# Adding a group's shared column back one group later, and running a graph network's three stages without barriers or queued weights between them

## The reference

```python
h = jnp.maximum(_layernorm(x), 0.0)
e_h = rel_embed[rel_id]
for W_r, W_sl, W_el in [(W_r1, W_sl1, W_el1), (W_r2, W_sl2, W_el2)]:
    self_msg = jnp.where(iso_mask[:, None], h @ W_el, h @ W_sl)
    agg = jax.ops.segment_sum((e_h + h[src]) @ W_r, dst, num_segments=3125)
    h = rrelu(agg * norm + self_msg)
x = x + h
h = jnp.maximum(_layernorm(x), 0.0)
qk, v = h @ Wqk + bqk, h @ Wv + bv
scores = jnp.clip(jnp.sum(qk[dst] * qk[src], axis=-1) / sqrt(128), -5.0, 5.0)
attn = segment_softmax(scores, dst)
out = jax.ops.segment_sum(attn[:, None] * v[src], dst, num_segments=3125) @ Wo + bo
x = x + gamma * layernorm(out + h) + beta
```

## Time and profile before

| | us |
|---|---|
| median of three runs | 870.51 (868.87 to 872.46) |
| the profiled execution | 870.01 |
| its span in the trace | 868.3 |
| TensorE busy | 732.6 |
| VectorE busy | 527.7 |
| ScalarE busy | 431.5 |
| GpSimd busy | 245.1 |

### The profile page before, as it was taken

The page is one execution under the profiler, slowest core; times in us unless marked ns, Lnnn a source line. Parts: engine busy times, 40 slices in busy tenths (PEclk is TensorE's granted clock), DMA queues, the critical chain, the costliest instruction groups (busy, mean ns, idle before and its releaser), DMA issues. The chain is left out here.

```text
span 868.3 us, 15380 instructions
## 1 busy us (share of the span) xinstructions
PE 732.6 (84%) x5767; PEld 545.2 (63%) x5767; DVE 527.7 (61%) x931; ACT 431.5 (50%) x1085; POOL 245.1 (28%) x273
## 2 busy tenths in 40 slices
PE   4266698898889898977399999859999999999993
PEld 3255587788778788866289999824444444444463
DVE  4987997786768677541033333414476767666676
ACT  0445765564555555551011111237767676767661
POOL 6130010000001111100000000026666666666662
PEclk9999799799989999987699999979999999999996
DMA  4100200033300000011311111130000000000000
GB/s 130 33 1 18 59 2 7 23 103 71 100 9 7 8 8 7 8 60 61 108 31 37 36 37 37 37 106 1 1 4 21 3 22 2 24 0 24 2 25 18
DMA packets 39763, 27.89 MB, mean 32 GB/s; under 512 B 5311, under 2 KB 38163, under 8 KB 39686
## 3 DMA queue, kind: packets, MB, share of 16 engines
q1 hardware_dynamic: 39206, 26.35, 10.5%
q10 hardware_dynamic: 480, 0.53, 0.2%
HBM read 13.28 MB, written 10.80 MB: 28 GB/s over the span
## 5 line engine op out<-in xcount | busy, mean ns | idle before, releaser
L1462 POOL TENSOR_TENSOR counts<-counts,work 125x500 f32<-125x500 f32 x150 | 162.3, 1082 | 97.5 <-DVE work L1526 84.1
L1016 PE MATMUL sums<-work 125*128 125x196 f16 (+15 forms) x1220 | 157.1, 256 | 24.7 <-DVE work L825 24.6
L1384 PE MATMUL a_ps_o<-work 125*128 125x500 f32 (+1 forms) x350 | 159.2, 545 | 7.1 <-DVE work L1530 6.7
L1526 DVE SCALAR_TENSOR_TENSOR work<-a_ps_s,counts 125x500 f32<-125x500 f32 x150 | 101.6, 677 | 93.5 <-ACT a_ps_s L1482 93.4
L1372 PE MATMUL a_ps_s<-work 128*125 128x500 f32 x300 | 152.0, 589 | 6.9 <-PEq L534 6.9
L819 DVE TENSOR_TENSOR work<-work,counts 125x3024 f16<-125x3024 f16 (+1 forms) x60 | 114.3, 1906 | 65.5 <-PE sums L1018 62.4
L1477 ACT ACTIVATE a_ps_s<-a_ps_s,work 125x500 f32<-125x500 f32 (+1 forms) x157 | 102.1, 650 | 86.5 <-PE a_ps_s L1372 83.4
L1018 PE MATMUL sums<-work 125*128 125x10 f16 (+15 forms) x800 | 133.7, 196 | 0.0
L1187 ACT CAST counts<-sums 128x364 f32 (+38 forms) x305 | 131.9, 472 | 2.1 <-issue 1.4
L977 PE MATMUL sums<-counts 125*128 125x250 f16 (+1 forms) x975 | 124.5, 275 | 10.0 <-ACT work L1129 10.0
L825 DVE TENSOR_TENSOR work<-work,counts 125x4200 f16<-125x4200 f16 (+15 forms) x120 | 125.5, 1086 | 0.0
(11 more groups left out here) (178 smaller groups left out, 703.3 us busy)
## 6 DMA issues: line engine op xcount, KB each, us to landing
first_columns<-counts SPq DMA_DIRECT2D x5, 610.4 KB
counts<-first_columns SPq DMA_DIRECT2D x5, 610.4 KB
counts<-counts SPq DMA_DIRECT2D x5, 468.8 KB
counts<-in_x SPq DMA_DIRECT2D x5, 312.5 KB
h_nodes<-counts SPq DMA_DIRECT2D x5, 312.5 KB
work<-in_x SPq DMA_DIRECT2D x12, 125.0 KB
x_after_messages<-work SPq DMA_DIRECT2D x12, 125.0 KB
h_attention<-work SPq DMA_DIRECT2D x12, 125.0 KB
```

The source lines that it names most:

```text
L1016: pe.matmul(win[:, 0:c, cols], lo[:, k * 2 * LO:k * 2 * LO + 128], m[:, k, h0 * w:(h0 + c) * w].rearrange("p (h d) -> p h d", d=w), start= ...
L1384: last = pe.matmul(ps_o[c % 2][:, 0:cols(u) // n], h3[:, j + i, :], pbuf[u % PB][:, i * NP:i * NP + cols(u) // n], start=j + i == 0, stop= ...
L1462: pool.tensor_tensor(a, a, p, ALU.add).then_inc(acc_done, 1)
L1526: dve.scalar_tensor_tensor(pbuf[u % PB], ps_s[u % 4][0:NP, 0:WIDE], float(np.exp(-CLIP)), counts[0:NP, j, c * WIDE:(c + 1) * WIDE], ALU.ma ...
```

## The change

There are two parts. **One:** on TensorE, `add_back(g - 1)` now stands behind the tiles of group g and ahead of that group's slots. ScalarE's loop, the slots and the waits for banks are as before. **Two:** the stages are joined. There is one program block and one PSUM tensor instead of two; attention's functions are called inside the first block. The last chunks of layer one are written in another order, chunk 11 has its own banks and `ht`, the two halves of each split are interleaved, and the rows from DRAM are asked for one batch earlier. The start of layer two's first chunk is done ahead of layer one's last `agg`. The weights of layer two are issued by ScalarE, and the five reloads of `counts` by SyncE behind each of layer two's first five chunks. Scores 0 to 3 and the first units start before the last chunk's rows are finished; `last_turn` and `last_qk` stand behind units 1 and 3.

```diff
@@ TensorE, groups
                     if q == n - 1:
                         last.then_inc(ring_free, 1)
+                    if g:
+                        add_back(g - 1)
                     for step in slots[g]:
                         layer1(*step)
-                    pe.wait_ge(carry_ready, g + 1)
-                    for win, h0, h1 in wins:
-                        last = pe.matmul(win[:, :, 0:1], ident_h[:, :], carry[:, g % 2, h0:h1, None], start=False, stop=True, skip_group_check=True)
-                    last.then_inc(summed, 1)
@@ TensorE, behind the groups
-            for step in slots[GROUPS]:
-                layer1(*step)
+            add_back(GROUPS - 1)
+            for kind, c in (("own", DIRECT + 1), ("agg", DIRECT), ("sum", DIRECT + 1), ("self", DIRECT + 1),
+                            ("rest", DIRECT + 1), ("own", LAST), ("agg", DIRECT + 1), ("sum", LAST), ("self", LAST), ("rest", LAST)):
+                for step in by_kind.pop((kind, c)):
+                    layer1(*step)
+            own(0, ORDER2[0])
+            sums(0, ORDER2[0], 0, EARLY).then_inc(early, 1)
+            layer1("agg", LAST, 0)
...
-            h3_turn(LAST, ORDER2[LAST])
-            qk(LAST, ORDER2[LAST])
+            pe.wait_ge(L["rows"], LAST)
+            A["tensor_first"](pe)
...
+            A["tensor"](pe, last_turn, last_qk)
@@ SyncE
-            sp.wait_ge(ring_free, len(BATCHES))
+            sp.wait_ge(ring_free, len(BATCHES) - 1)
...
-            sp.wait_ge(sums_done, CHUNKS)
-            for i in range(5):
-                v = slice(5 * i, 5 * i + 5)
-                sp.dma_start(counts[0:NP, v, 0:HEAD], heads.rearrange("p (j d) -> p j d", d=HEAD)[:, v, :]).then_inc(heads_in, 16)
...
-            for t, v in zip((wr, ws[:, 0:D], ws[:, D:]), weights2):
-                sp.dma_start(t, v).then_inc(L["wts"], 16)
...
                 sp.dma_start(h3[:, c * LB * D:(c + 1) * LB * D], xc.rearrange("p b f -> p (b f)")).then_inc(L["h3_out"], 16)
+                if i < 5:
+                    v = slice(5 * i, 5 * i + 5)
+                    sp.dma_start(counts[0:NP, v, 0:HEAD], heads.rearrange("p (j d) -> p j d", d=HEAD)[:, v, :]).then_inc(heads_in, 16)
@@ ScalarE, ahead of layer two
+            act.wait_ge(agg_done, CHUNKS)
+            for t, v in zip((wr, ws[:, 0:D], ws[:, D:]), weights2):
+                act.dma_start(t, v).then_inc(L["wts"], 16)
+            act.dma_start(wqk, wqk_d).then_inc(L["wts"], 16)
+            act.dma_start(bqk, bqk_d.rearrange("(p o) -> p o", o=1)).then_inc(L["wts"], 16)
@@ ScalarE, behind layer two
+            A["scalar_first"](act)
             act.wait_ge(L["x2_ready"], CHUNKS)
@@ attention, TensorE: unit u
+            if u == 1:
+                last_turn()
+            if u == 3:
+                last_qk()
```

More of the change, by code:

```diff
@@ L326, in messages @@
     hn_in = [sem(f"hn_in{i}") for i in range(4)]
[L327 removed]
+    rounded2, parts2_ready = ([sem(f"{n}{i}") for i in range(2)] for n in ("rounded2_", "parts2_ready"))
+    early = sem("early")
     slots, at_slot = plan()
@@ new lines, in score @@
+    def score(pe, u):
+        c, j, n = units[u]
+        if u == NB - 1:
+            pe.wait_ge(T["rows"], -(-NB // 2))
+        out = ps_s[u % 4]
+        if c < FULL:
+            last = pe.matmul(out[0:NP, :WIDE], qk_t[:, j * NP:(j + 1) * NP], qk_t[:, c * WIDE:(c + 1) * WIDE], start=True, stop=True)
+        else:
+            for i in range(n):
+                last = pe.matmul(out[0:NP, i * NP:(i + 1) * NP], qk_t[:, (j + i) * NP:(j + i + 1) * NP], qk_t[:, FULL * WIDE:], start=True, stop=True)
+        last.then_inc(scores, 1)
@@ new lines, in below, with exponent, scalar_first @@
+    def below(act, u):
+        act.wait_ge(scores, u + 1)
+        s = ps_s[u % 4][0:NP, 0:cols(u)]
+        act.activation(s, s, ACT.Relu, bias=five, scale=-float(D) ** -0.5).then_inc(limited, 1)
+    def exponent(act, u):
+        act.wait_ge(limited, u + 1)
+        s = ps_s[u % 4][0:NP, 0:cols(u)]
+        act.activation(s, s, ACT.Exp, bias=five, scale=-1.0).then_inc(exped, 1)
+    def scalar_first(act):
+        act.wait_ge(consts, 2)
+        below(act, 0)
+        below(act, 1)
+        exponent(act, 0)
@@ new lines, in run_scalar, with take @@
+    def run_scalar(act, last_turned, last_rows):
+        def take(c):
+            act.wait_ge(pv_done, end_unit(c))
+            if c:
+                act.wait_ge(f_done, c)
+            w = blocks(c) * NP
+            act.copy(hv[:, 0:w], ps_o[c % 2][:, 0:w]).then_inc(hv_out, 1)
+        for u, (c, j, n) in enumerate(units):
+            if 0 < u < len(units) - 1:
+                below(act, u + 1)
+            if u:
+                exponent(act, u)
+            if u == 1:
+                last_turned()
+            if u == 3:
+                last_rows()
+            if c == 0 and j == 14:
+                act.wait_ge(wv_turned, 1)
+                act.copy(wv_t, ps_f[:, 0:D]).then_inc(wv_t_out, 1)
+            if c == 0 and j == 17:
+                act.wait_ge(wvo_done, 1)
+                act.copy(wvo, ps_f[:, D:2 * D]).then_inc(wvo_out, 1)
+                act.copy(bvo, ps_f[0:NP, 2 * D:3 * D]).then_inc(wvo_out, 1)
+            if 0 < c < FULL and j == 1 or c == FULL and j == 0:
+                take(c - 1)
+        take(FULL)
```

639 lines of the change are left out of this document (325 added, 314 removed).

## The result

| | before | after |
|---|---|---|
| median of the runs, us | 870.06 (868.87 to 872.46) | 876.42 (875.25 to 876.97) |
| the profiled execution | 870.01 | 876.65 |
| its span | 868.3 | 874.9 |
| last set of tiles and the add-back behind it | 372.5 | 399.9 |
| layer two's first weight product | 431.2 | 436.0 |

A forecast was written before the change was run, and what follows sets the result against it. TensorE, busy 732.6 of 868.3 us, was taken as the bound, so gains had to come from its idle time or slow stretches. The terms: 870.0 + 15 + 10 − 25 − 6 = 864 us, range 848 to 880.

The forecast's parts named there:

- The reloads of `counts`, at no cost: Layer two's first five chunks: each reload holds SyncE 3.9 us, covered by over 8 us of TensorE work per chunk.
- last rival: Layer two: reloads collide with x loads, five chunks lose 2 us each, 874 us in all; 4 in 100.
- 15 us lost: Edge stage: longer TensorE waits for ScalarE at 10 `agg` and 11 first `sum`, 0.7 us each, between 11 and 18.
- The carry's round trip between ScalarE and TensorE does not get more cover: Edge stage: one group's tiles and slots stand between add-backs before and after, only in the other order; no time counted.
- 10 us lost: Edge stage: the clock falls at four of eight chunk boundaries, 2.5 us each; from nothing to 28 us.
- 25 us gained: Passage from layer one into layer two: first weight product sooner after joining the stages and issuing weights earlier; 22 to 28.
- the 2.5 us taken off: Layer two's weights: possible shortening of the earlier 5.4 us, as reloads no longer share DMA engines; arrival taken as 407.
- The 1 us added for a clock that had been down for longer: Start of layer two: 1 us gained because TensorE idles 3 us instead of 15 there.
- 6 us gained: Passage into attention: first weighted sum 10.8 us earlier, less 0.8, 3.0 and 1.0 us; from 4 to 9.
- the forecast waits of units 2 and 4: Attention's start: ScalarE, in order, stands behind `last_turn` and `last_qk`, costing 1.6 us at unit 2 and 1.4 at unit 4.
- The clock falls at every boundary: slower: Edge stage rival: a fall at each `agg` and following `sum`, 20 to 28 us, total 878 (873 to 882); 20 in 100.
- 12, 18 and two thirds of 46: Chances summed for below 866 us: part one costs nothing (12), clock holds (18), own case of falls at some boundaries (46).

The follow-up runs named there:

- run 4: The changed kernel with each reload of `counts` issued behind the x load of the next iteration instead of ahead of it: 863.8 us, ratio 0.992.
- run 6: The changed kernel with the add-back in its old place and each reload of `counts` behind the next iteration's x load: 835.6 us, ratio 0.960.
- run 3: The changed kernel with `own`, the sums and `agg` of each chunk one group later, add-back still late: 848.5 us, ratio 0.974.
- run 9: run 8 with the late add-back of the changed kernel and each chunk's steps one group later as in run 3: 850.8 us, ratio 0.979.
- run 8: run 7 with 14 filler products on TensorE at each of 21 waits for a first sum or `agg`: 832.0 us, ratio 0.957.
- run 5: The changed kernel with 24 filler products of 128 columns on TensorE ahead of each of the 21 first-sum and `agg` waits: 861.3 us, ratio 0.990.
- run 1: The changed kernel with the add-back in its old place, behind its own group's tiles and slots; passages stay changed: 845.6 us, ratio 0.970.
- run 7: run 6 with the last chunk's leftovers of layer two (`last_qk`, ScalarE's last copy and rows) moved later in attention: 833.6 us, ratio 0.958.

## Why the prediction was wrong

- **The reloads of `counts`, at no cost** is the step that failed most. They cost 7.1 us in the changed kernel's trace, and 8 to 10 by runs 4 and 6. The prediction saw what can happen as its last rival, "five chunks lose 2 us each because x lands behind 625 KB: 874", and gave it 4 in 100. Its cover was reckoned in the issue time of SyncE, 3.9 us each, but the issue took 0.35 us, and it is the transfer that x stood behind. VectorE got x only 6.8 us after its issue, and that used up the slack between VectorE and the next chunk's `h3_turn`: four of the five chunks lost 1.6 to 2.8 us there. Runs 4 and 6, where the order of the two issues is turned, have these waits no more.
- **15 us lost** by waits was right: 13.7, at the places and for the reason given. Run 3 undid it as the mechanism says.
- **"The carry's round trip between ScalarE and TensorE does not get more cover"**, with nothing taken off or put on for it, missed that it loses some. ScalarE stands 4.2 to 6 us at its register loads, once in 20 groups ("issue" in the rows). It starts them behind the copy of the group before, which now comes one set of tiles later. So an add-back that waited until 82.04 waits until 84.29. ScalarE's copies behind the three sets of loads come at 61.05, 84.05 and 111.08 us instead of 59.69, 81.80 and 107.09: 1.4, 2.3 and 4.0 us late. The first chunk's first sum comes at 118.87 us instead of 114.32, 4.1 us of it not in the waits counted above. That the loads are what makes the delay grow is read from these rows; no run moved them. Other small waits of the stage are 1.6 us less, so 2.5 us were missing. The place is as late in run 9, with the late add-back, and early in run 8, with the early one (filler ahead of that sum at 118.1 and 114.1). The rows, of the changed kernel and of the one before by turns:

```profile
111.08 0.18 ACT L1239 CAST work<-sums 128x27 f16 x1 [5.68 <-issue]
```

```profile
107.09 0.18 ACT L1179 CAST work<-sums 128x27 f16 x1 [5.41 <-issue]
```

```profile
84.29 0.23 PE L1027 MATMUL sums<-work,ident_h 128*128 128x27 f16 x1 [5.72 <-ACT work L1239]
```

```profile
82.04 0.23 PE L1026 MATMUL sums<-work,ident_h 128*128 128x27 f16 x1 [5.43 <-ACT work L1179]
```

```profile
118.87 1.43 PE L997 MATMUL sums<-counts 125*128 125x250 f16 x6 [1.23 <-ACT work L1189]
```

```profile
114.32 0.81 PE L977 MATMUL sums<-counts 125*128 125x250 f16 x6 [0.79 <-ACT work L1129]
```

- **10 us lost** by the clock was right in size: the stage's 27.4 us less 13.7, 4.1 and −1.6 leave 11.2, and the busy time at the lower clock gives 12.8 at most. Some 2 us of these have nothing to do with a boundary: the clock was still low from the start until 123.6 us. It is low again from 140.7 to 144, 171 to 182, 202 to 209, 229 to 236, 304.5 to 311, 328 to 332, 352 to 363 and 379.6 to 383 us; six of the ten boundaries have a fall, and a pair of 1.74 and 1.71 us at 278 and 282 has none. Run 5 shows that the falls cost and aren't just seen beside the waits.
- **25 us gained** into layer two was 22.6. Chunk 11's `own` waited for the last copy until 403.82 and its sums began at 405.81, 5.9 us behind the last tiles where 6.0 were reckoned (378.5 − 372.5), and the first weight product came 36.1 us behind them instead of 34.5. The 75 sums of chunk 11 took 10.36 us where 8.5 were reckoned, the first 4 us at the lower clock, so `agg` came 18.6 us behind the last tiles instead of 17.0. In run 1 they took 9.08 us, and there the passage gained 25.2 with the same 2.3 us of `issue`. These idle times are not the cause: without them the product would have waited for the weights until 435.4, 0.6 us less. The weights' 4 us from the last issue to the product, of which no run shows the 2.5 us taken off, were 2.9; the last issue came 33.2 us behind the last tiles where 30.5 were reckoned. The 1 us added for a clock that had been down for longer doesn't show.
- **6 us gained** into attention was 5.3, by the forecast waits of units 2 and 4, 1.50 and 1.44 us for the 1.6 and 1.4 given.

The terms as measured: 870.0 + 13.7 + 2.5 + 11.2 − 22.6 + 7.1 − 5.3 = 876.6. That it comes out is no proof of the parts, since the 11.2 are what the other terms leave of the stage. Against the prediction's 864 that is 12.6 us more: 7.1 the reloads, 2.5 the register loads, 3.1 the passages, and −1.3 and 1.2 the waits and the clock. By these terms it would have been 869.5 without the reloads, no difference from before (run 4 took 863.8, with 5 us less of the edge stage by the clock in its trace). The rival "The clock falls at every boundary: slower" came near the time, 878, but not by its cause: the clock cost 11 us more than before, not 24. (The chances of "faster" were added wrongly: 12, 18 and two thirds of 46 are 61 in 100, not 59.)

## What to carry to other kernels

When a release is moved past a consumer's slot, count what stands between the release and each wait behind it, not only what stands between two releases. A large prefetch on the queue of a small load that is needed at once belongs behind the small load; its price is its transfer, not its issue. And a wait of under 2 us in a busy TensorE can cost more than it lasts: filler there, where it waits anyway, was worth 15 us in run 5; where it hardly waited (run 9) filler made the stage longer. Real work in those places (run 3) was worth 28 us.

The fastest kernel here, run 7 (833.6 us, and run 8 that can't be told from it), takes part two of the change without part one, with each reload behind x.

## What I had not expected of the hardware

- The clock's falls differ between executions of one program. Run 7's executions are 826.7 once and 833.3 to 834.7 six times; run 4's are three at 860.5 to 861.1 and three at 866.6 to 868.9. Where traces show both, as in run 7 against run 6, 6 us of the edge stage go with the clock.
- The low clock of the first 110 us is without effect on the time: run 9 had the upper clock from the start on, its order's first sum was as late as in the changed kernel (118.92 and 118.87 us).
